# Split weights stored to DRAM in the first quarter and loaded in the other three, in a four-stage residual kernel with another opening order

## The reference

```python
x = x + einsum('bct,bcd->bdt', x, L0_weights[subject])          # x: (64, 64, 512)
x = x + einsum('bct,bcd->bdt', x, L1_weights[adapter])
x = x + einsum('bct,bcd->bdt', x, L2_weights[adapter]) + bias[adapter][:, :, None]
gate = x @ Wg + (x @ Ag[adapter]) @ Bg[adapter]                 # Wg, Wu: (512, 2048)
up   = x @ Wu + (x @ Au[adapter]) @ Bu[adapter]
h = silu(gate) * up
x = x + h @ Wd + (h @ Ad[adapter]) @ Bd[adapter]                # Wd: (2048, 512), rank 16
```

## Time and profile before

| | |
|---|---|
| median of 3 executions | 1345.86 us (1345.44 to 1346.74) |
| the profiled execution, whole | 1347.3 us |
| its span, first to last instruction | 1345.5 us |
| PE busy | 1316.3 us, 98% |
| DVE / ACT / POOL busy | 994.4 / 549.2 / 629.4 us |
| mean granted TensorE clock | 0.991 |
| DMA | 197.00 MB, mean 146 GB/s |

### The profile page before, as it was taken

One profiled execution on the slowest core, in us unless ns is written; L12 is line 12 of the kernel. 1 busy time (PEld: TensorE's weight loads), 2 busy tenths in 40 slices (PEclk: granted clock), 3 DMA queues, 4 the chain that ended last, 5 costly groups with the idle time before them and its releaser, 6 DMA issues.

```text
span 1345.5 us, 17990 instructions
## 1 busy us (share of the span) xinstructions
PE 1316.3 (98%) x6402; PEld 1095.5 (81%) x6402; DVE 994.4 (74%) x1530; ACT 549.2 (41%) x940; POOL 629.4 (47%) x531
## 2 busy tenths in 40 slices
PE   8699999999999999999999999999999999999998
PEld 7478888888888888888888888888887888888886
DVE  5776688777787667788678767777877876777765
ACT  3444444444334335444334334444433334433331
POOL 2256565455405545555431655554542444444440
PEclk8799999999999999999999999999999999999999
DMA  4445354445636334555383534444446432333321
GB/s 168 157 136 198 109 176 141 153 142 165 232 148 211 122 102 132 158 169 150 113 316 114 184 103 144 147 150 130 152 176 250 153 98 83 106 99 114 114 78 63
DMA packets 105687, 197.00 MB, mean 146 GB/s; under 512 B 10368, under 2 KB 54656, under 8 KB 105600
## 3 DMA queue, kind: packets, MB, share of 16 engines
q1 hardware_dynamic: 83328, 125.06, 28.6%
q0 software_dynamic: 22272, 70.80, 16.3%
HBM read 160.69 MB, written 35.13 MB: 146 GB/s over the span
## 4 chain that ended last, share of the span: by engine, by line
PE 88%; DVE 6%; DMA 1%; POOL 1%; issue 1%; ACT 1%; SPq 0%; ACTq 0%; DVEq 0%; POOLq 0%
PE px L1104 26%; PE pd L1104 25%; PE py L1104 12%; PE pz L1104 6%; PE pv L1104 6%; PE pz L1120 4%; PE py L1120 2%; PE px L1120 2%; PE pd L1322 2%; DMA w_raw<-w_gu 1%; DVE wg_lo L844 1%; PE pd L1131 1%; DVE h_lo L1006 1%; DVE acc L1001 1%; PE pd L1177 1%
## 5 line engine op out<-in xcount | busy, mean ns | idle before, releaser
L496 POOL DMA_INDIRECT b_got<-b_table,idx_b x256 | 257.4, 1006 | 288.2 <-PE py L1120 204.5
L514 POOL TENSOR_TENSOR h_lo<-g,h_hi 128x512 fp32r<-128x512 f32 x128 | 176.4, 1378 | 334.0 <-ACT h_hi L586 332.8
L977 DVE TENSOR_TENSOR acc<-pd,acc 128x512 f32<-128x512 f32 x256 | 174.7, 690 | 82.1 <-PE pd L1104 81.7
L1104 PE MATMUL px<-xo_hi,wg_hi 128*128 128x512 f32 x544 | 222.9, 410 | 11.8 <-ACT g L586 5.7
L586 ACT ACTIVATE wg_hi<-w_raw 128x512 fp32r<-128x512 f32 (+1 forms) x272 | 155.6, 573 | 169.6 <-PE py L1120 94.5
L844 DVE TENSOR_TENSOR wg_lo<-w_raw,wg_hi 128x512 fp32r<-128x512 f32 (+1 forms) x272 | 198.1, 733 | 34.6 <-ACT wg_hi L586 33.8
L1104 PE MATMUL px<-xo_hi,wg_lo 128*128 128x512 f32 x544 | 213.5, 392 | 0.0
L1104 PE MATMUL px<-xo_lo,wg_hi 128*128 128x512 f32 x544 | 213.5, 392 | 0.0
L1104 PE MATMUL pd<-wd_hi,h_hi 128*128 128x512 f32 x512 | 203.1, 397 | 1.0 <-POOL h_lo L514 0.9
L1104 PE MATMUL pd<-wd_lo,h_hi 128*128 128x512 f32 x512 | 199.4, 389 | 0.0
L1104 PE MATMUL pd<-wd_hi,h_lo 128*128 128x512 f32 x512 | 199.3, 389 | 0.0
(11 more groups left out here) (213 smaller groups left out, 2327.2 us busy)
## 6 DMA issues: line engine op xcount, KB each, us to landing
w_raw<-w_gu SPq DMA_DIRECT2D x68, 512.0 KB, 3.7
wd_raw<-w_dn SPq DMA_DIRECT2D x64, 320.0 KB, 3.0
xo_hi<-xops SPq DMA_DIRECT2D x21, 512.0 KB, 8.2
xo_lo<-xops SPq DMA_DIRECT2D x21, 512.0 KB, 9.9
acc<-x SPq DMA_DIRECT2D x8, 1024.0 KB, 8.3
out<-acc SPq DMA_DIRECT2D x7, 1024.0 KB, 4.6
xops<-st_hi SPq DMA_DIRECT2D x24, 256.0 KB, 2.8
xops<-st_lo SPq DMA_DIRECT2D x24, 256.0 KB, 2.9
```

Of the source, the lines that this page charges most:

```text
L496: gp.indirect_dma_start(out=dst, out_offset=None, in_=rows_of, in_offset=bass.IndirectOffsetOnAxis(ap=rows.bitcast(U32), axis=0)).then_inc ...
L514: return gp.tensor_tensor(dst, src_raw, src_hi, ALU.subtract)
L977: ins = dve.tensor_tensor(dst, pd[j][:, :], dst, ALU.add)
L1104: ins = pe.matmul(psum, w_parts[wi], x_parts[xi], start=(start and i == 0), stop=(stop and i == 2), skip_group_check=more)
```

## The change

Three parts.

1. Two DRAM tensors hold the split parts: `wg_parts` for each of the 17 units (1.835 MB each) and `wd_parts` for each of the 16 blocks (0.66 MB each). In quarter 0 the weights are loaded raw, summed and split as before, and then stored (`store_weights`, `store_down`). In quarters 1 to 3 there are no raw loads, no sums and no splits of weights: SP loads the parts straight to `wg` and `wd` (`load_parts`, `load_down_parts`), each group as soon as the last product that reads it is done. ACT waits, before it overwrites a group in quarter 0, until the group's store has landed (`w_out`, `dn_out`).
2. In quarters 1 to 3 the subtractions that POOL made (`h_low`, three of the tokens' low parts) are made by DVE. In unit -1 `select` comes ahead of all of `finish`.
3. The opening is ordered anew, and the first unit's operations on ACT and DVE are written out, mixed with the split of the tokens. The adapter and bias loads go out from ACT; the first raw weights come ahead of x; the first table sum comes ahead of seven of eight picks; warm-ups are 14 and 4 where there were 10 and 14, and 9 and 4 more stand inside unit -1. In block 1 the first two `down_high` stand behind the copy of S2's bank.

The core of the diff:

```diff
+HIGH_ORDER = (S1, A22, S2, S3, S4)
+LOW_ORDER = (S1, S2, S3, S4, A22)
...
-WARM_UP = (10, 14, 10)
+WARM_UP = (14, 4, 9, 4)
...
+    wg_parts = nc.dram_tensor("wg_parts", (UNITS, P, 2, 7, WH), F32).ap()
+    wd_parts = nc.dram_tensor("wd_parts", (BLOCKS, P, 2, DOWN_COLS), F32).ap()
...
-        wg_hi = sb("wg_hi", [P, 7, WH], F32R)
-        wg_lo = sb("wg_lo", [P, 7, WH], F32R)
+        wg = sb("wg", [P, 2, 7, WH], F32R)
...
+            def store_weights(n, g):
+                lo, hi = GROUPS[g]
+                sp.wait_ge(w_done[g], n + 1)
+                sp.dma_start(wg_parts[n, :, :, lo:hi, :], raw(wg[:, :, lo:hi, :])).then_inc(w_out[g], 16)
+
+            def load_parts(n, g):
+
+                lo, hi = GROUPS[g]
+                sp.wait_ge((p5_mm, p2_mm, p3_mm, p4_mm)[g], n)
+                sp.dma_start(raw(wg[:, :, lo:hi, :]), wg_parts[n % UNITS, :, :, lo:hi, :]).then_inc(w_in[g], 16)
+
+            def store_down(b):
+                sp.wait_ge(dn_done, b + 1)
+                sp.dma_start(wd_parts[b], raw(wd[:, b % 2])).then_inc(dn_out[b % 2], 16)
+
+            def load_down_parts(q, b):
+
+                d = phase(q, b // 2, 0) - 1
+                for half in range(2):
+                    if q == 1 and b == 0:
+                        sp.wait_ge(dn_out[half], SUPER * 16)
+                    if half:
+                        sp.wait_ge(down_mm, 5 * (d + 1))
+                    else:
+                        sp.wait_ge(down_half, d + 1)
+                    sp.dma_start(raw(wd[:, half]), wd_parts[b + half]).then_inc(parts_in[half], 16)
...
-            sp.dma_start(ints[:, 1, :], adapter.partition_broadcast(P)).then_inc(ints_in, 16)
             sp.dma_start(w2_four, w2_rows.rearrange("p (j n) -> p j n", j=TP)).then_inc(e0_in, 16)
             sp.dma_start(w1_four, w1_pairs.rearrange("p (j n) -> p j n", j=TP)).then_inc(e0_in, 16)
-            sp.dma_start(bias_src, bias_pairs).then_inc(bias_in, 16)
+
+            sp.wait_ge(ints_in, 2 * 16)
+            sp.wait_ge(e0_in, 2 * 16)
+            load_weights(0)
             load_x(0, 0)
-            load_weights(0)
             load_x(0, 1)
             load_b(0)
...
+            for g in range(4):
+                store_weights(0, g)
+            sp.wait_ge(o_done, LOW_ORDER.index(S4) + 1)
...
+                if q and b % 2 and b > 0:
+                    load_down_parts(q, b - 1)
+                parts = not splits(n) and n + 1 < QUARTERS * UNITS
+                if parts and b < BLOCKS - 1:
+                    load_parts(n + 1, 0)
...
-                if b >= 1 and b % 2 and b + 1 < BLOCKS:
-                    load_down(blocks_done(q, b))
-                    load_down(blocks_done(q, b) + 1)
+                if q == 0 and b >= 1 and b % 2:
+                    store_down(b - 1)
+                    store_down(b)
+                    if b + 1 < BLOCKS:
+                        load_down(b + 1)
+                        load_down(b + 2)
...
+                        if k in (S1, A12, S4, A22):
+                            g = (S1, A12, S4, A22).index(k)
+                            if q == 0:
+                                sp.wait_ge(w_out[g], UNITS * 16)
+                            load_parts(n + 1, g)
+                elif parts:
+                    for g in range(1, 4):
+                        load_parts(n + 1, g)
+                elif splits(n):
+                    for g in range(4):
+                        store_weights(n + 1, g)
+                    if n + 2 < UNITS:
+                        next_weights(n)
...
-                h_low(q, b, 0)
+                if q == 0:
+                    h_low(q, b, 0)
...
+                if n:
+                    act.wait_ge(w_out[g], n * 16)
...
+            sum_high(S1, o_s1_sum)
+            keep_s1(0)
+            copy(xo_hi[:, A22, :], a2_raw[1]).then_inc(o_hi, 1)
+            sum_high(S2, o_s2_sum)
+            keep_s5(0)
+            sum_high(S3, o_s3_sum)
+            weights_high(1, 0)
+            sum_high(S4, o_s4_sum)
+            keep_s2(0)
+            ua_high(0, 0, 0)
+            act.wait_ge(p2_mm, 1)
+            weights_high(1, 1)
+            b_high(1)
+            ua_high(0, 1, 1)
+            ua_high(0, 0, 1)
+            weights_high(1, 2)
+            act.wait_ge(p4_mm, 1)
+            copy(g1[:, :], px[:, :]).then_inc(c21_kept, 1)
+            ua_high(0, 1, 0)
+            weights_high(1, 3)
...
+                if (q, b) == (0, 1):
+                    down_high(0)
+                    down_high(1)
+                if splits(n) and b <= 1:
...
-            for p in range(TP):
-                picks(p)
+            picks(0)
             dve.wait_ge(e2_done, 1)
             dve.wait_ge(oe_mm, 1)
             dve.tensor_tensor(es_four[:, :, C:2 * C], four(pv[:, 0:TP * C]), e2_four, ALU.add).then_inc(oe_add, 1)
-            for p in range(TP, QP - 1):
+            for p in range(1, TP + 2):
                 picks(p)
+            sums(0)
             picked(0)
-            picks(QP - 1)
-            sums(0)
+            for p in range(TP + 2, QP):
+                picks(p)
             dve.wait_ge(eb_done, 1)
             o_combine(0)
-            picked(1)
-            block_numbers()
             for g in (0, 2, 1, 3):
                 weights_low(0, g)
+            picked(1)
+            b_low(0)
+            block_numbers()
             dve.wait_ge(eb_done, 2)
             o_combine(1)
-            b_low(0)
             tables()
...
-            selectors(0, 0)
             for j in range(TP):
                 dve.wait_ge(o_a1_hi, j + 1)
                 ins = dve.tensor_tensor(
@@ -924,7 +1025,10 @@
                     xo_hi[:, A11:A12 + 1:2, :].rearrange("p k (c n) -> p k c n", c=2)[:, :, :, j * P:(j + 1) * P],
                     ALU.subtract)
             ins.then_inc(o_a1_done, 1)
+            sums(1)
             for i in range(2):
+                if i:
+                    selectors(0, 0)
                 both = [a.rearrange("p (c n) -> p c n", c=2)[:, :, 2 * i * P:2 * (i + 1) * P] for a in (s_raw[S1], *a2_raw)]
                 dve.wait_ge(o_a2_kept, 2 * (i + 1))
                 dve.tensor_tensor(both[0], both[1], both[2], ALU.add).then_inc(o_s1_sum, 1)
@@ -943,8 +1047,6 @@
                 dve.tensor_tensor(of_pair(s_raw[S4], j), chunks(pd[j][:, WH:2 * WH]), of_pair(s_raw[S2], j), ALU.subtract
                                   ).then_inc(o_s4_sum, 1)
             o_low(S3, s_raw[S3])
-            o_low(S4, s_raw[S4])
-            o_low(A22, a2_raw[1])
...
+            c11(0)
+            o_low(S4, s_raw[S4])
+            o_low(A22, a2_raw[1])
+            ua_low(0, 0, 0, 1)
+            u3(0)
+            weights_low(1, 0)
+            c12(0)
+            weights_low(1, 1)
+            ua_low(0, 1, 1, 2)
+            ua_low(0, 0, 1, 3)
+            weights_low(1, 2)
+            ua_low(0, 1, 0, 4)
+            select(0, 0)
+            weights_low(1, 3)
+            selectors(0, 1)
...
+            picked(range(TP + 2))
+            o_combine(0)
+            picked(range(TP + 2, QP))
+            o_layers(0)
             pe.wait_ge(bias_done, 1)
-            o_combine(0)
-            o_layers(0)
             o_combine(1)
             for j in range(TP):
                 pe.wait_ge(o_layer_a, j + 1)
                 turn(0, 0, j, pd[j]).then_inc(o_turn, 1)
-            pe.wait_ge(eb_done, 2)
...
+                if first:
+                    for a in range(2):
+                        first_turn(a)
+                weights_ready(n, 0)
...
-                    for a in range(TP):
+                    for a in range(2, TP):
                         first_turn(a)
                     pe.wait_ge(o_layer_a, QP)
                     pe.wait_ge(w_done[1], 1)
                     product(pz, A12, True, True).then_inc(p2_mm, 1)
+                    pe.wait_ge(o_a2_kept, TP)
+                    warm_up(WARM_UP[2], pv)
```

232 lines of the change are left out of this document (132 added, 100 removed).

## The result

The changed kernel took 1449.14 us (median of 4, 1445.07 to 1451.24) beside 1346.3 (1345.44 to 1347.64) for the kernel before: ratio 1.0759, 95% interval 1.0734 to 1.0785. It is 7.6% slower where 1.1% faster was forecast.

A forecast was written before the change was run, and what follows sets the result against it. PE, busy 98% of the span, was taken to bound the kernel. Terms -15.1 - 1.1 + 4.0 - 2.0 = -14.2 us gave 1331.7 us from 1345.86; 8-in-10 range 1326.5 to 1342.

The forecast's parts named there:

- Storing in quarter 0: Quarter 0: raw loads queue behind stores on SP, PE waits 1.0 us in four units; +4.0 us, bounds 0 to +12.
- Rival 3: Quarter 0: stores to DRAM run at half the loads' rate; +33 us instead of +4, 1361 us; chance 0.06.
- Rival 2: Quarter 0: SP late in each of 15 units, or 3 us in the four; +8 more, 1340 us; chance 0.14.
- Opening, A: Start to first layer: earlier adapter numbers and picks bring the first layer to 18.1 from 25.25 us; -7.1 us.
- B and C: First layer to S1, then to block 0: S1 at 35.0, block 0 at 48.9 us; cumulative -9.5, then -15.1.
- Rival 1: Opening, unit -1: the clock falls there too, products at double spacing; +4 to +5 us, 1336 us; chance 0.15.
- Block 1's S2: Block 1: PE's 1.14 us wait for ACT goes, as two down splits move behind the bank copy; -1.1 us.
- Loading in quarters 1 to 3: Quarters 1 to 3: part loads at about 241 GB/s arrive in time, so PE does not wait; 0 us.
- a sign of being wrong: Listed as showing the forecast wrong: PE waits on a transfer of wg or wd.
- 1 us late in each of 50 units: Quarters 1 to 3: price if part loads lose their cover; +50 us.
- PE takes no notice of traffic itself: Matmul pace: 4.80 records a us at 406 GB/s against 4.83 at 158 GB/s, so traffic costs PE nothing.
- Boundaries: Quarters' starts: PE's waits on up, u and h_lo shrink, with select before finish; -2.0 us, bounds 0 and -4.

The follow-up runs named there:

- opening-only: Changed kernel's opening alone, small loads on SyncE: weights split in all four quarters, no parts stored or loaded; 1341.61, 1340.92 and 1341.3 us in three jobs.
- on time: State of some timing sessions, signals not delayed at gathers: the unaltered changed kernel took 1374.16 and 1371.56 us.
- the moved line: Changed kernel with small loads on SyncE, plus quarter 0's raw load issued ahead of the last group's parts store; 1449.14 us.
- ScalarE's order: Changed kernel, but in quarter 0 ScalarE copies the S2 product out before splitting the first group's weights; 1447.72 us.
- the run with one store: Changed kernel with small loads on SyncE, storing only the first unit's parts and those of blocks 0 and 1; 1420.61 us.
- third job: One timing session repeating unaltered kernels: changed kernel 1374.16 us, with small loads on SyncE 1374.35, kernel before 1345.74.
- late state: State of some timing sessions, signals delayed while gathers run: the unaltered changed kernel took 1449.14 and 1456.78 us.
- my first experiment: Changed kernel with its adapter and bias loads issued by SyncE instead of ScalarE; 1376.09 us, ratio 1.0228.

## Why the prediction was wrong, step by step

**Storing in quarter 0 (+4.0, bounds 0 to +12): the step that failed in every job.** Changed kernel against opening-only, on time: 334.63 - 300.83 = 33.8 us; in medians 1374.16 - 1340.92 = 33.2. The mechanism named (raw load behind the stores on SP, first split behind it on ACT, the copy of S2's bank behind that, PE waiting) is right, as the moved line, ScalarE's order and the run with one store show. Its size was not. PE's waits on the copy in the four units forecast to pay, those after parts (blocks 7, 9, 11, 13), on time:

```profile
213.08 0.47 PE L1242 MATMUL px<-xo_hi,wg 128*128 128x512 f32 x1 [1.97 <-ACT up L652]
...
256.25 0.47 PE L1242 MATMUL px<-xo_hi,wg 128*128 128x512 f32 x1 [1.83 <-ACT up L652]
...
298.93 0.60 PE L1242 MATMUL px<-xo_hi,wg 128*128 128x512 f32 x1 [2.67 <-ACT up L652]
...
342.17 0.77 PE L1242 MATMUL px<-xo_hi,wg 128*128 128x512 f32 x1 [5.12 <-ACT up L652]
```

They come to 11.6 us in place of 4 x 1.0. Two more such waits are in block 4 (1.23) and block 2 (5.61, below), 6.8 us in place of nothing; of block 2 the prediction said that it "comes out just even". Block 2 on time, SP's issues and what waited for the last:

```profile
86.08 2.32 SPq L403 DMA_DIRECT2D wd_parts<-wd  x2
...
88.44 1.39 SPq L388 DMA_DIRECT2D wd_raw<-w_dn  x2
...
89.88 3.14 SPq L393 DMA_DIRECT2D wg_parts<-wg  x4
...
93.18 0.92 SPq L377 DMA_DIRECT2D w_raw<-w_gu  x1
...
106.57 0.42 DVE L935 TENSOR_TENSOR w_raw<-w_raw 128x256 f32<-128x256 f32 x1 [9.00 <-DMA w_raw<-w_gu]
...
107.02 0.63 ACT L652 ACTIVATE wg<-w_raw 128x512 fp32r<-128x512 f32 x1 [6.77 <-DVE w_raw L935]
...
107.56 0.58 ACT L652 ACTIVATE up<-px 128x512 f32<-128x512 f32 x1
...
108.28 0.77 PE L1242 MATMUL px<-xo_hi,wg 128*128 128x512 f32 x1 [5.61 <-ACT up L652]
```

The raw load lands 13.4 us after its issue. Ahead of it stand 1.31 MB of down parts, 0.66 of raw down weights and 1.84 of parts, 3.8 MB, and the gathers take their share of the same 21 us:

```profile
86.00:107.00 21.00, 16.67 (x68) 13.70 (x66) 7.47 (x12) 3.36 (x6) 13.04 (x12) 0.83 0.89 325
```

I had counted the down parts' 1.31 MB but let only the units after token parts pay, took the other eleven for free, and left out the 2 MB of gathers every second unit. The rate was 325 GB/s, not the 406 of the earlier trace rows.

The waits are not the whole loss. From block 0's first product to the ruler's last row of quarter 0, first the opening-only kernel (third job), then the changed kernel on time:

```profile
57.28:347.81 290.53, 287.50 (x1401) 238.84 (x1401) 215.97 (x323) 127.31 (x220) 157.49 (x128) 1.00 0.48 150
```

```profile
56.60:380.93 324.33, 300.18 (x1401) 247.26 (x1401) 208.32 (x318) 125.07 (x218) 156.96 (x128) 0.95 0.72 249
```

PE is idle 24.1 us instead of 3.0, and the same 1401 multiplications keep it busy 12.7 us longer, with the granted clock at 0.95 instead of 1.00. So of 33.8 us, 21.1 are waits and 12.7 the clock, which this term of the prediction had at nothing. In the window of block 2 above the clock is at 0.83. Within a microsecond of the waits of 1.97, 2.67, 5.12 and 5.61 us the products come 0.43 us apart, at the lower of the two clock levels; after those of 1.23 and 1.83 they stay at 0.23.

Rival 3 has nearly the size (+33), by another mechanism. Stores of parts land as fast as loads of them (512 KB each, on time), while the raw load's median went from 3.7 us to 5.4:

```profile
wg<-wg_parts SPq DMA_DIRECT2D x153, 512.0 KB, 4.3
...
wg_parts<-wg SPq DMA_DIRECT2D x51, 512.0 KB, 4.3
...
w_raw<-w_gu SPq DMA_DIRECT2D x17, 512.0 KB, 5.4
```

Rival 2's "3 us in the four" has those four units nearly right (2.9 each), but neither the other two nor the clock.

**Opening, A (-7.1 forecast).** Timeline of the changed kernel on time (against the earlier trace rows):

```profile
9.52 1.90 PE L1362 MATMUL pz<-vacc,g 128*128 128x64 f32 x16
...
18.01 2.08 PE L1371 MATMUL pv<-acc 128*128 128x128 f32 x8 [3.03 <-DMA acc<-w_rows,idx_w]
...
23.19 5.07 PE L1380 MATMUL pd<-acc 128*128 128x512 f32 x8
...
34.97 0.47 PE L1242 MATMUL px<-xo_hi,wg 128*128 128x512 f32 x1
...
41.60 0.47 PE L1242 MATMUL py<-xo_hi,wg 128*128 128x512 f32 x1 [0.74 <-DVE xo_lo L964]
...
56.60 0.58 PE L1242 MATMUL px<-xo_hi,wg 128*128 128x512 f32 x1
```

The picks start at 9.52, earlier even than the 10.1 forecast, and then PE waits 3.03 us, until 18.01, for gathered subject rows. The chain had no gathers in it. Their issue begins at 6.80 and the fourth goes out at 11.37 (before: 8.02 and 12.28):

```profile
6.80 1.11 POOL L560 DMA_INDIRECT acc<-w_rows,idx_w  x1 [5.13 <-DVE idx_w L894]
...
11.37 0.94 POOL L560 DMA_INDIRECT acc<-w_rows,idx_w  x1 [0.31 <-issue]
```

The first layer starts at 23.19 instead of the forecast 18.1, and runs at the lower clock level (5.07 us for what took 3.67; the clock is 0.60 from 18 to 28 us, 1.00 before). A is worth 2.1 us against the execution of the earlier trace rows, and 0.2 against the one of the same job (23.42).

**B and C (-9.5, -15.1 in all).** The first product comes at 34.97 (28.6), S1 at 41.60 (35.0), block 0 at 56.60 (48.9; before 64.00, or 62.23 in the same job): -7.4 in all, or -5.6. Of the 7.7 us missing against 48.9, 5.1 are A's; the hand-made rest was right to 2.6. Rival 1, a lower clock in the opening, came true in part: the clock is 0.92 from 40 to 60 us, and the first products of block 0 are 0.43 apart.

**Block 1's S2 (-1.1).** Worth nothing. The wait on ACT's g is gone in the opening-only kernel, but PE waits a little later for a low part of POOL:

```profile
88.59 0.73 PE L1217 MATMUL pd<-wd,h_hi 128*128 128x512 f32 x2 [1.19 <-POOL h_lo L565]
```

From block 0's first product to the end of quarter 0 that kernel takes 290.53 us, the kernel before 290.28 (64.00 to 354.28). What its quarter 0 gains by the ruler (300.83 against 302.72) lies ahead of block 0.

**Loading in quarters 1 to 3 (0).** Right with signals on time: 960.11 against 960.54, and at the forecast traffic, 244 GB/s where 241 was worked out. PE did wait 3.8 us on part loads, which the prediction had named as a sign of being wrong, while its idle time from 345 to 1320 us stayed at 3.9, under the 4 forecast:

```profile
345.00:680.00 335.00, 332.92 (x1614) 277.59 (x1613) 181.91 (x282) 97.63 (x162) 95.80 (x94) 0.99 0.75 244
```

In the result's job it is the largest term, 69.5 us. Against the changed kernel on time, with the same 4647 multiplications, 50.6 of 70.0 us are idle time (54.5 against 3.9) and 19.4 the clock (0.98 against 1.00 over the stretch). Part loads are not what is late in it (3.0 us of waits on wg). The forecast's price, "1 us late in each of 50 units", had the size but for another reason. The step rested on "PE takes no notice of traffic itself", which holds for its pace on time (956.2 us busy in quarters 1 to 3, 956.4 before); its signals do take notice, in some jobs, while gathers and part loads are in flight. No row shows it: the one burst with 406 GB/s there was on time.

**Boundaries (-2.0).** By quarters 1 to 3 of the ruler, -0.4 and -1.8 in the two traces of the changed kernel on time, and -0.1 and -0.2 in the two with the small loads on SyncE: mostly not there.

Sum on time, within the third job: 5.6 gained to block 0, 33.9 lost from there to the end of quarter 0, 0.4 gained after: +27.9, the spans' 1371.8 - 1343.9. In the result's job: 1.1 gained to the first sum, 35.4 lost in quarter 0, 69.5 after: +103.9, the spans' 1449.4 - 1345.5. My range ended at 1342, so the prediction fails without the late state too; with it, it fails by 107 us.

## What to carry to other kernels

Work taken off engines that nobody waits for buys nothing (DVE's busy time in quarters 1 to 3 fell from 717 to 498 us, and the time by 0.4); what such a change adds to a queue that issues in one order is paid by the one load behind it that someone needs. Count for that load every byte issued or gathered since the queue was last empty, at the rate of a mixed stretch, and price what a wait does to the clock after it, here 12.7 us beside 21.1 of waits. Time a kernel whose traffic doubles in more than one job before believing either a gain or a cause: my first experiment "proved" a culprit that a repeat of the unchanged kernel cleared.
